# Exponentials ahead of the output's evacuation in the second attention's ScalarE order

## The reference

```
q, k, v = x @ Wq, x @ Wk, x @ Wv        # 32 query heads, 8 key heads, 16 wide
q, k = rope(q), rope(k)
scores = q @ k.T / 4, causal            # 512 x 512 for each sequence and head
attn = softmax(scores)
ctx = attn @ v                          # 512 x 16 for each head
out = ctx @ Wo
```

## Time and profile before

| what | value |
|---|---|
| median of 3 runs | 1342.86 us (1341.97 to 1346.67) |
| the profiled execution: its own time | 1345.62 us |
| the profiled execution: its span | 1343.8 us |
| PE busy in the span | 1215.2 us (90%) |
| ACT busy | 748.7 us (56%) |
| DVE busy | 821.2 us (61%) |
| POOL busy | 522.2 us (39%) |
| the stretch with the loop over slots | about 1005 to 1223 us of the span |

### The profile page before, as it was taken

The page is one execution under the profiler, slowest core; times in us unless marked ns, Lnnn a source line. Parts: engine busy times, 40 slices in busy tenths (PEclk is TensorE's granted clock), DMA queues, the critical chain, the costliest instruction groups (busy, mean ns, idle before and its releaser), DMA issues. The chain is left out here.

```text
span 1343.8 us, 20915 instructions
## 1 busy us (share of the span) xinstructions
PE 1215.2 (90%) x6674; PEld 1047.5 (78%) x6674; DVE 821.2 (61%) x2543; ACT 748.7 (56%) x1717; POOL 522.2 (39%) x475
## 2 busy tenths in 40 slices
PE   4879999999999999999975999997869999998595
PEld 3768888888888888888763888785759999996484
DVE  5466776667766777667774222223548888884455
ACT  4356765566655666566642454202149999994220
POOL 3244554345543454444300233202336666662200
PEclk9889999999999999999998899998889999998797
DMA  4211111111101111010001122101021111110101
GB/s 148 87 32 46 34 33 32 27 40 32 40 25 34 32 32 40 25 32 25 1 1 40 46 71 70 32 0 57 16 61 33 48 45 47 46 28 1 60 1 62
DMA packets 30428, 52.47 MB, mean 39 GB/s; under 512 B 5744, under 2 KB 6128, under 8 KB 30320
## 3 DMA queue, kind: packets, MB, share of 16 engines
q1 hardware_dynamic: 28592, 48.25, 12.5%
q10 hardware_dynamic: 1728, 2.88, 0.6%
HBM read 39.58 MB, written 2.10 MB: 31 GB/s over the span
## 5 line engine op out<-in xcount | busy, mean ns | idle before, releaser
L322 POOL TENSOR_TENSOR turned<-turned,sin 128x512 f32<-128x512 f32 x80 | 103.5, 1293 | 357.3 <-ACT turned L229 357.3
L244 ACT ACTIVATE probs<-probs,neg_max 128x256 f32<-128x256 f32 x256 | 126.6, 500 | 7.9 <-DVE neg_max L392 7.9
L1068 ACT ACTIVATE a_probs<-a_probs,a_neg_max 128x512 f32<-128x512 f32 (+3 forms) x256 | 123.6, 575 | 0.0
L325 POOL TENSOR_TENSOR turned<-turned,by_cos 128x512 f32<-128x512 f32 x80 | 112.2, 1403 | 7.3 <-DVE by_cos L366 1.2
L1205 DVE CUSTOM_DVE_ANT_0 a_probs<-bank,a_mask 128x512 f32<-128x512 f32 (+3 forms) x256 | 109.7, 484 | 1.2 <-PE bank L1280 1.1
L81 PE MATMUL bank<-wo_hi,oT_hi 128*128 128x512 f32 x256 | 100.4, 392 | 9.9 <-DVE oT_lo L449 9.9
L486 PE MATMUL bank<-xT_hi,wq_hi 128*128 128x512 f32 x256 | 100.7, 393 | 3.0 <-DVE by_cos L366 3.0
L486 PE MATMUL bank<-xT_lo,wq_hi 128*128 128x512 f32 x256 | 100.7, 393 | 0.0
L486 PE MATMUL bank<-xT_hi,wq_lo 128*128 128x512 f32 x256 | 99.9, 390 | 0.0
L81 PE MATMUL bank<-wo_hi,oT_lo 128*128 128x512 f32 x256 | 99.8, 390 | 0.0
L81 PE MATMUL bank<-wo_lo,oT_hi 128*128 128x512 f32 x256 | 99.7, 389 | 0.0
(11 more groups left out here) (227 smaller groups left out, 3584.3 us busy)
## 6 DMA issues: line engine op xcount, KB each, us to landing
staged<-weights SPq DMA_DIRECT2D x80, 256.0 KB, 2.7
f_staged<-weights_f SPq DMA_DIRECT2D x33, 256.0 KB, 2.7
a_q_stack<-a_qT_hi SPq DMA_DIRECT2D x64, 64.0 KB, 2.0
rows<-x_T ACTq DMA_DIRECT2D x8, 256.0 KB, 5.6
rows<-x_rows SPq DMA_DIRECT2D x1, 2048.0 KB, 9.9
a_k_stack<-a_kT_hi SPq DMA_DIRECT2D x64, 32.0 KB, 2.0
a_q_stack<-a_qT_lo SPq DMA_DIRECT2D x32, 64.0 KB, 2.0
out<-rows SPq DMA_DIRECT2D x8, 256.0 KB, 2.9
```

The source lines that it names most:

```text
L244: act.activation(probs[:, s % 2, h, :], probs[:, s % 2, h, :], ACT.Exp, bias=neg_max[:, s % 2, h:h + 1], scale=SCALE0, accum_out=row_sum[: ...
L322: pool.tensor_tensor(turned[:, a % 2, :], turned[:, a % 2, :], sin[:, :], ALU.mult).then_inc(sin_done, 1)
L325: pool.tensor_tensor(turned[:, a % 2, :], turned[:, a % 2, :], by_cos[:, a % 2, :], ALU.add).then_inc(roped, 1)
L1068: act.activation(row_probs(s, qt), row_probs(s, qt), ACT.Exp, bias=neg_max[:, h, qt:qt + 1], scale=-1.0).then_inc(exp_done, 1)
```

## The change

In ScalarE's loop the call of `exps` for the next slot is moved ahead of the call of `evacuate`. No instruction is added, removed or resized, and no other engine's list changes.

```diff
             for s in range(SLOTS1 + 2):
                 u, h = divmod(s, GROUP1)
+                if s + AHEAD_EXPS < SLOTS1:
+                    exps(s + AHEAD_EXPS)
                 if s % 2 == 1 and s >= 3:
                     evacuate((s - 3) // 2)
-                if s + AHEAD_EXPS < SLOTS1:
-                    exps(s + AHEAD_EXPS)
                 if s < SLOTS1:
                     high_turned(s)
                 if h == 2 and 2 <= u + 1 < UNITS1:
```

## The result

| | before | changed |
|---|---|---|
| median of six executions each (three of before's six are the three behind 1342.86) | 1344.17 us (1341.66 to 1350.19) | 1357.68 us (1351.80 to 1361.06) |
| ratio, with its 95% interval | | 1.0081 (1.0059 to 1.0104) |
| the profiled execution: its own time, its span | 1345.62, 1343.8 us | 1352.47, 1350.6 us |
| first copy of turned probabilities to last evacuation | 214.48 us | 221.73 us |

The changed kernel is slower, by 0.8% in this comparison, where 0.41% was forecast: 1357.68 us lies outside the range. The two profiled executions stand only 6.85 us apart, and all of that is in the loop over slots, which is 7.25 us longer (the last row of the table). So two questions follow.

A forecast was written before the change was run, and what follows sets the result against it. ScalarE was taken to bind, at 6.54 and 6.68 us a pair. Ring +5.6, head -0.4 and end +0.3 made +5.5 us on the median 1342.86: 1348.4 us, own range 1344.5 to 1352.5, whole range 1343.0 to 1353.0.

The forecast's parts named there:

- a hidden 0.11 us in every second pair: In ScalarE's loop, the evacuation's wait for matmuls held by GpSimd's split; the move removes it, worth 1.5 us at most.
- the new wait of `apply` for the evacuation: TensorE's next apply into the same bank waits for the later evacuation and begins 0.67 us later than before.
- the ring: Evacuation, apply, output turned, scores, turn, copy, high parts, exponentials, evacuation: at least 6.81 us a pair, 5.6 us in all.
- the alternation with the copy of v: In every second pair ScalarE's copy of v, 0.14 us, lies on the ring too: 6.95 us instead of 6.81.
- the copy L1075 of even slots as the place where ScalarE pays: ScalarE idle or a widened spacing, about 0.27 us, ahead of this copy in even passes, released by the transposes L1298.
- The rival in which ScalarE still binds: Loop over slots: TensorE merely shifts inside its slack, ScalarE's 6.54 and 6.68 us bind; 1341.0 us, not slower; chance 0.12.
- The rival of the clock: In the loop, TensorE loses its 2.4 GHz clock or can't catch up: 1355 to 1363 us; chance 0.10.
- 0.67: Delay in us of TensorE's apply, paid by each of 30 pairs if TensorE couldn't use its slack: 20 us.
- the 3.8 us for a pair at the lower clock: Cost for each pair hit if TensorE's clock fell to 1.2 GHz, doubling its part of the ring.
- The head: Loop's start, up to slot 4's copy: exponentials fill ScalarE's wait for TensorE, a gain of 0.4 us.
- the end: Loop's end, slots 61 on, without scores: +0.3 us for a last evacuation held by a later apply.
- A scatter of about 1.5 us in a median: Allowance for noise in the measured whole-kernel time, part of the forecast's own range, 1344.5 to 1352.5 us.

## Why the prediction was wrong

**The mechanism held.** The binding engine (ScalarE, with a hidden 0.11 us in every second pair), the new wait of `apply` for the evacuation, the ring with its eight links, the alternation with the copy of v, the copy L1075 of even slots as the place where ScalarE pays: each is in the trace where the text had it, and the runs with three exponentials ahead and with the transposes off the ring show that the ring is the cost. The rival in which ScalarE still binds is out: the loop is 6 to 7 us longer in all five profiles. The rival of the clock is not seen: 1.00 from 1028 to 1209 us each time, with TensorE's recorded busy share at 97%. TensorE also caught up: it stood ready before each late evacuation, and paid 0.27 a pair and not 0.67. (That rival's price was also too high as written: the 3.8 us for a pair at the lower clock count the 0.65 from the evacuation to the apply, most of which is ScalarE's; TensorE's links in the ring, 1.36 + 0.35 + 0.72 + 0.70, come to 3.1.)

**The step that failed first: the ring was mis-sized by 0.07 us.** "Whatever slack each engine has, a pair can't be shorter than the ring: ... = 6.81." It measured 6.88. No single link is to blame: apply 1.39 for 1.36, scores reached after 0.36 for 0.35, turn to copy 0.71 for 0.70, copy 0.49 for 0.48, exponentials 1.82 for 1.81. One waiting apply stood in the earlier trace rows with 1.38 (1127.68 to 1129.06), and I took the 1.36 of the other; but which link is long changes from pair to pair. In the next pair, with the copy of v, the apply comes 0.69 after the evacuation (1134.87 to 1135.56) and has 1.36 itself, and the sum is again 0.07 too long. Why links in a ring are a few hundredths longer than the same spacings outside it is not shown. The excess over 6.68 that I multiplied was only 0.20 a pair, so 0.07 is a third of it: 28 x 0.27 = 7.6 in place of 5.6. The head gave 0.33 for 0.4; the end, where I had put +0.3, gave nothing. In the profile that is 7.25 us for 5.5, too small by a quarter.

**The step that failed by more: the scatter.** "A scatter of about 1.5 us in a median." The median of before that I started from, 1342.86 of three executions, is 2.5 us under the 1345.36 of the 107 with a recorded clock; the six of the changed kernel came out 5.2 above the 1352.53 of its 38. The three parts make up the whole miss: 1348.4 + 2.5 for the start, + 1.7 for the ring (the medians of all executions stand 7.2 apart, not 5.5), + 5.2 for the six is 1357.8, where 1357.68 was measured. Single executions of before have a standard deviation of 3.2 us, those of the changed kernel 4.0, and most of it goes with the granted clock. Both medians were trusted to a microsecond or two. That the six of the changed kernel had low clocks was bad luck as far as is known: no run shows that the change lowers the clock, and over all executions the two mean clocks differ by 0.0009 with a standard error of 0.0007. With 38 and 107 executions the change costs 7.7 us, or 6.9 at equal clock: 0.5 to 0.6%, between the forecast 0.41% and the measured 0.81%, and just over the 0.5% that divided "same" from "slower". The profiles' own times, 1345.62 and 1352.47, were a better pair to compare than the medians, since both had a mean clock of 0.953.

## What to carry to other kernels

When two engines both look busy all the time, add up the ring that a buffer with one copy closes through both of them: each link from start to start, with the waits' own latency. An order costs nothing while that ring is shorter than the binding engine's own work, and its whole excess, once a round, from there on; so here a move was free for three exponentials and cost 8 us for the fourth. And where single executions scatter with the clock by more than the effect, compare the stretch in the trace, or the times at equal clock.

## What the runs showed that I had not expected

The mean granted clock of an execution goes with most of the scatter in its time: 1.0 us for each 0.001, with 1.3 us (one standard deviation) left over, in a kernel whose loop runs at a granted clock of 1.00 from 1020 us on in every profile. And ScalarE's instructions are recorded longer in the runs where it waits least, at the same spacing. The evacuation lasts 0.60 to 0.63 us in the kernel before and 0.70 with three exponentials ahead, from the fourth on. With one ahead it grows along the loop, by about 0.04 us a pair, from 0.60 to 1.10 in the first 14, and then stays at 1.04 to 1.14; the last two, with no exponentials in their pass, have 0.60. In each, 0.47 to 0.50 us pass to the next instruction. ScalarE's timeline with one ahead:

```profile
1125.34 1.17 ACT L1068 ACTIVATE a_probs<-a_probs,a_neg_max 128x512 f32<-128x512 f32 x1
1125.95 1.04 ACT L1085 ACTIVATE a_oT_now<-bank 128x512 f32<-128x512 f32 x1
1126.43 1.75 ACT L1068 ACTIVATE a_probs<-a_probs,a_neg_max 128x384 f32<-128x384 f32 x3
```

The length of a record is no price here; the spacing is. What stretches the record was not tried.
